# Spreading the base projection over 24 attention passes and turning the second LoRA block in pass 11

## The reference, cut to what matters

```python
qk = (x @ Wqk_w.T + Wqk_b).reshape(b, n, H, E, 2)          # H = 8 heads of E = 8
scores = jnp.einsum('bhqd,bhkd->bhqk', q, k)
attn = jax.nn.softmax(scores, axis=-1) / HEAD_DIM ** 0.5
out = jnp.einsum('bhsl,bhlv->bhsv', attn, v)
...
h = jnp.einsum('nd,erd->ner', x_flat, A)                    # 8 experts of rank 16
hw = h * combine[:, :, None]
expert_out = jnp.einsum('ner,eor->no', hw, B) * SCALING
base_out = x_flat @ W_base.T + b_base
out = base_out + expert_out
```

## Time and profile before

| what | value |
|---|---|
| time, median of three runs | 1461.27 us (1458.69 to 1462.09) |
| the profiled execution: its time, its span | 1458.69 us, 1456.6 us |
| busy over the span | PE 1370.9, DVE 980.3, ACT 855.1, POOL 633.5 us |
| passes 0 to 31, from 78 to 211 us | 133 us, of which PE 121.8, DVE 83.2, ACT 79.8, POOL 49.4 us busy |
| granted clock of PE in that stretch | 0.94 on the mean |

### The profile page before, as it was taken

How to read it: one execution, slowest core, us unless ns; L and a number is a source line. 1 busy time by engine, 2 the same in 40 slices (tenths; PEclk the granted TensorE clock), 3 DMA queues, 4 the chain that set the end, 5 groups by cost and what they waited for, 6 DMA issues and landing times.

```text
span 1456.6 us, 21333 instructions
## 1 busy us (share of the span) xinstructions
PE 1370.9 (94%) x7350; PEld 1075.4 (74%) x7350; DVE 980.3 (67%) x1834; ACT 855.1 (59%) x2103; POOL 633.5 (43%) x973
## 2 busy tenths in 40 slices
PE   4989897999999999999999999999999999989997
PEld 3743345788888788877888888788878877768786
DVE  6666655677777777768777777767677777675333
ACT  2355564566666666666666657666666666563211
POOL 4333345444454454434454544544344545433211
PEclk9999888999999999999999999999999999999999
DMA  4200032001110020102011100201020012114010
GB/s 142 66 1 1 2 100 69 30 1 59 36 40 31 30 67 9 39 22 74 5 56 35 39 31 30 68 7 45 16 74 20 26 35 38 38 59 136 15 58 29
DMA packets 35882, 61.01 MB, mean 42 GB/s; under 512 B 9056, under 2 KB 13280, under 8 KB 35776
## 3 DMA queue, kind: packets, MB, share of 16 engines
q1 hardware_dynamic: 35776, 59.66, 13.0%
HBM read 49.68 MB, written 9.96 MB: 41 GB/s over the span
## 4 chain that ended last, share of the span: by engine, by line
PE 75%; DVE 12%; issue 7%; ACT 3%; POOL 2%; DMA 1%; POOLq 0%; DVEq 0%; SPq 0%; ACTq 0%
PE T L2302 7%; PE T L1917 7%; PE T L1919 6%; PE T L1918 6%; PE S L1919 5%; PE S L1918 5%; PE S L1917 5%; PE VB L1919 4%; PE VB L1917 4%; PE WB L1917 4%; PE VB L1918 4%; PE WB L1919 4%; PE WB L1918 4%; PE VB L2073 2%; PE T L2185 2%
## 5 line engine op out<-in xcount | busy, mean ns | idle before, releaser
L892 POOL TENSOR_TENSOR RI<-SM,C 128x1 f32<-128x1 f32 x256 | 143.3, 560 | 506.6 <-ACT PB L1222 505.4
L1689 DVE CUSTOM_DVE_ANT_0 PB<-S,REL,SLC 128x128 f32<-128x128 f32 (+7 forms) x256 | 204.4, 813 | 80.1 <-PE S L1919 78.5
L1222 ACT ACTIVATE PB<-PB,NM 128x128 f32<-128x128 f32 (+7 forms) x256 | 198.9, 777 | 69.0 <-DVE NM L1689 64.1
L1295 ACT ACTIVATE R<-T 128x512 fp32r<-128x512 f32 x288 | 170.6, 593 | 100.4 <-PE T L2302 98.4
L893 POOL TENSOR_SCALAR PB<-PB,RI 128x128 f32<-128x128 f32 (+7 forms) x256 | 214.9, 839 | 25.2
L1696 DVE TENSOR_TENSOR R<-T,R 128x512 fp32r<-128x512 f32 x288 | 197.4, 688 | 42.2 <-ACT R L1295 23.7
L2302 PE MATMUL T<-C,PB 128*128 128x128 f32 x1152 | 176.6, 276 | 12.0 <-DVE R L1696 6.8
L2302 PEld LDWEIGHTS T<-C,PB 128*128 128x128 f32 x1152 | 134.1, 140 | 48.1 <-DVE R L1696 18.1
L1202 ACT ACTIVATE JUNK<-WB 128x128 bf16<-128x128 f32 x252 | 66.2, 277 | 92.5 <-PE WB L1919 92.5
L1917 PE MATMUL T<-R 128*128 128x512 f32 x256 | 103.9, 406 | 4.0 <-issue 2.2
L1919 PE MATMUL T<-R 128*128 128x512 f32 x256 | 100.4, 392 | 0.0
(11 more groups left out here) (295 smaller groups left out, 3513.7 us busy)
## 6 DMA issues: line engine op xcount, KB each, us to landing
RAW<-w SPq DMA_DIRECT2D x86, 256.0 KB, 2.8
DQ<-codes SPq DMA_DIRECT2D x16, 352.0 KB, 3.5
DQ<-absmax SPq DMA_DIRECT2D x16, 352.0 KB, 3.0
dequantised<-DQ SPq DMA_DIRECT2D x16, 352.0 KB, 2.2
PB<-x SPq DMA_DIRECT2D x12, 256.0 KB, 3.2
PB<-dequantised SPq DMA_DIRECT2D x5, 512.0 KB, 4.6
PB<-x_scratch SPq DMA_DIRECT2D x8, 256.0 KB, 4.0
out<-PB SPq DMA_DIRECT2D x8, 256.0 KB, 2.0
```

The lines of the kernel that those rows point to most:

```text
L892: ch.link(e.tensor_tensor(RI[:, k:k + 1], SM[:, k:k + 1], C[:, C_EXP + 5:C_EXP + 6], ALU.pow))
L1222: e.activation(pb(m, a, 0, L), pb(m, a, 0, L), ACT.Exp, scale=-1.0, bias=NM[:, k:k + 1], accum_out=SM[:, k:k + 1]).then_inc(exp_done, 1)
L1295: e.activation(r(PT + AT[i, ("PV", kb)] % 3 * 1024, 512), T[AT[known, it] % 2][:, :], ACT.Copy).then_inc(t_act, 1)
L1689: e.tensor_tensor_reduce(out=pb(m, a, 0, L), in0=bank[:, 0:L], in1=REL[:, TOK - L:TOK], scale=SLC[:, a:a + 1], scalar=3.0e38, op0=ALU.add, ...
```

## The change

The base projection was packed more densely into passes 0 to 5, and blocks 3 to 7 followed three passes each until pass 20. Now each block takes three passes from the start, with 5, 5 and 2 pieces, and the last one ends in pass 23. XB moves from pass 0 to pass 11, which has no pieces, and from bank VB to bank WB, between the blocks 3 and 4. The first PV waits only for group 0. Two items of the merged list stand ahead of ST 1 and the rest behind it, and this holds for the head items from pass 24 on as well. SH moves to the end of its pass. The gating of block t-1 on POOL moves to HN t, and that of the last block from pass 22 to pass 24.

```diff
@@ -100,26 +100,16 @@
 EARLY = 4
 W_AT = {}
-for _x in [("F", t) for t in range(NT)] + [("WO", t) for t in range(NT)] + [("PQ", 1)]:
+for _x in ([("F", t) for t in range(EARLY)] + [("XB", 0)] + [("F", t) for t in range(EARLY, NT)] + [("WO", t) for t in range(EARLY)]
+           + [("WO", t) for t in range(EARLY, NT)] + [("PQ", 1)]):
     W_AT[_x] = len(W_AT)
-FILL_X = 22
+FILL_X = 24
 BASE_PRE = 6
...
-FILL = {0: (_pieces(0, 6, 7), _pieces(0, 8, 9, 10, 11)),
-        1: ([("HN", 0)], _pieces(1, 0, 1, 2)),
...
-for _t in range(3, NT):
-    FILL[3 * _t - 3] = _pieces(_t, 0, 1), _pieces(_t, 2, 3, 4)
-    FILL[3 * _t - 2] = _pieces(_t, 5, 6), _pieces(_t, 7, 8, 9)
-    FILL[3 * _t - 1] = _pieces(_t, 10, 11), [("HN", _t)]
+_b = [("B", 0, m) for m in range(3 * KT)]
+FILL = {0: _b[BASE_PRE:10], 1: _b[10:] + [("HN", 0)], 11: [("XB", 0)]}
+for _t in range(1, NT):
+    _b, _x = [("B", _t, m) for m in range(3 * KT)], 3 * _t - (1 if _t < EARLY else 0)
+    FILL.update({_x: _b[:5], _x + 1: _b[5:10], _x + 2: _b[10:] + [("HN", _t)]})
...
@@ unit_items
-    pre, post = FILL.get(x, ([], []))
+    fill = FILL.get(x, []) + head_items(x - EARLY_X)
     first, second, extra = couples(x) if x <= 23 else (None, None, None)
     seq = [("ST", 0)] + ([first] if first else []) + ([("PV", x - 1)] if x else [])
-    seq += pre + [("ST", 1)] + ([second] if second else []) + ([("XB", 0)] if x == 0 else [])
-    if x in (7, 15, 23):
-        return seq + [("SH", x // NT + 1)] + post + head_items(x - EARLY_X)
-    return seq + post + head_items(x - EARLY_X) + ([extra] if extra else [])
+    seq += fill[:2] + [("ST", 1)] + ([second] if second else []) + fill[2:] + ([extra] if extra else [])
+    return seq + ([("SH", x // NT + 1)] if x in (7, 15, 23) else [])
@@ POOL
                         add_bias0(it[1])
-                    elif it[0] == "B" and it[1] and it[2] == 7:
-                        gate0(it[1] - 1)
+                        if it[1]:
+                            gate0(it[1] - 1)
@@ high_hn (ACT)
-                act.wait_ge(xa_full, g + 1)
-                e.activation(r(OT + g * 1024, 512), VB[:, :], ACT.Copy).then_inc(xa_high, 1)
+                if g == 0:
+                    act.wait_ge(xa_full, 1)
+                else:
+                    act.wait_ge(w_full, W_AT["XB", 0] + 1)
+                e.activation(r(OT + g * 1024, 512), (VB, WB)[g][:, :], ACT.Copy).then_inc((xa_high, xb_high)[g], 1)
@@ low_hn (DVE)
-                dve.wait_ge(xa_high, g + 1)
+                dve.wait_ge((xa_high, xb_high)[g], 1)
                 o = OT + g * 1024
-                e.tensor_tensor(r(o + 512, 512), VB[:, :], rf(o, 512), ALU.subtract).then_inc(xa_low, 1)
+                e.tensor_tensor(r(o + 512, 512), (VB, WB)[g][:, :], rf(o, 512), ALU.subtract)\
+                    .then_inc((xa_low, w_free)[g], 1)
@@ values0, turn_hn (PE)
                 if x == 0:
-                    pe.wait_ge(xa_low, 2)
+                    pe.wait_ge(xa_low, 1)
...
                 if g == 1:
-                    pe.wait_ge(xa_low, 1)
+                    pe.wait_ge(w_free, W_AT["XB", 0])
                 pe.wait_ge(hn_ready, 4 * g + 4)
                 for t in range(4):
-                    last = e.transpose(VB[:, t * P:(t + 1) * P], HN[:, (4 * g + t) * P:(4 * g + t + 1) * P], IDENT)
-                last.then_inc(xa_full, 1)
+                    last = e.transpose((VB, WB)[g][:, t * P:(t + 1) * P], HN[:, (4 * g + t) * P:(4 * g + t + 1) * P], IDENT)
+                last.then_inc((xa_full, w_full)[g], 1)
```

More of the change, by code:

```diff
@@ L102 @@
 W_AT = {}
-for _x in [("F", t) for t in range(NT)] + [("WO", t) for t in range(NT)] + [("PQ", 1)]:
+for _x in ([("F", t) for t in range(EARLY)] + [("XB", 0)] + [("F", t) for t in range(EARLY, NT)] + [("WO", t) for t in range(EARLY)]
+           + [("WO", t) for t in range(EARLY, NT)] + [("PQ", 1)]):
     W_AT[_x] = len(W_AT)
-FILL_X = 22
+FILL_X = 24
 BASE_PRE = 6
-def _pieces(t, *ms):
-    return [("B", t, m) for m in ms]
-FILL = {0: (_pieces(0, 6, 7), _pieces(0, 8, 9, 10, 11)),
-        1: ([("HN", 0)], _pieces(1, 0, 1, 2)),
[L115 to L118, removed]
-for _t in range(3, NT):
-    FILL[3 * _t - 3] = _pieces(_t, 0, 1), _pieces(_t, 2, 3, 4)
-    FILL[3 * _t - 2] = _pieces(_t, 5, 6), _pieces(_t, 7, 8, 9)
-    FILL[3 * _t - 1] = _pieces(_t, 10, 11), [("HN", _t)]
+_b = [("B", 0, m) for m in range(3 * KT)]
[3 more added lines that the diff above has]
+    FILL.update({_x: _b[:5], _x + 1: _b[5:10], _x + 2: _b[10:] + [("HN", _t)]})
 PAIRS = 16
@@ L548, in program @@
         xa_low = sem("xa_low")
+        xb_high = sem("xb_high")
         m_high = sem("m_high")
@@ L1152, in sums0 @@
                 if u == 3:
-                    act.wait_ge(xa_full, 2)
+                    act.wait_ge(w_full, W_AT["XB", 0] + 1)
                 e.activation(SUMS[u], VB[:, :], ACT.Copy).then_inc(sums_ready, 1)
@@ L2079, in turn_hn @@
                 if g == 1:
-                    pe.wait_ge(xa_low, 1)
+                    pe.wait_ge(w_free, W_AT["XB", 0])
                 pe.wait_ge(hn_ready, 4 * g + 4)
                 for t in range(4):
-                    last = e.transpose(VB[:, t * P:(t + 1) * P], HN[:, (4 * g + t) * P:(4 * g + t + 1) * P], IDENT)
-                last.then_inc(xa_full, 1)
+                    last = e.transpose((VB, WB)[g][:, t * P:(t + 1) * P], HN[:, (4 * g + t) * P:(4 * g + t + 1) * P], IDENT)
+                last.then_inc((xa_full, w_full)[g], 1)
             def experts(t):
-                pe.wait_ge(xa_low, t // 4 + 1)
+                if t < EARLY:
+                    pe.wait_ge(xa_low, 1)
+                else:
+                    pe.wait_ge(w_free, W_AT["XB", 0] + 1)
                 pe.wait_ge(split, W0_EXP)
```

## The result

| kernel | median of 5 runs | profiled execution | its span | mean granted clock |
|---|---|---|---|---|
| before | 1458.69 us (1457.42 to 1462.09) | 1458.69 us | 1456.6 us | 0.985 |
| changed | 1468.36 us (1464.19 to 1469.68) | 1465.94 us | 1464.0 us | 0.984 |

The changed kernel is slower: ratio 1.0053, 95% interval 1.0037 to 1.0069. The forecast was 1461.7 us with a range up to 1465. The profiled spans differ by 7.4 us. The summary page doesn't say where: busy PE is 1373.5 us (1370.9 before), and the mean clock is the same. So I lined up the start of PV in every pass. The table has the distance from one PV to the next where the two kernels differ, in us; row x ends at the PV of pass x.

The account below looks back on a forecast made before the run. It took PE, busy 94% of the span, and its handovers with DVE to bound the kernel. Terms summed to -0.9 us, plus 1.3 for the clock in pass 11: +0.4, 1461.7 us, range 1458.0 to 1465.0.

Parts of the forecast that it names:

- the clock in pass 11: Around pass 11, without 128x128 matmuls except transposes: a short fall to half clock more likely than not, +1.3 us (0 to +2.5).
- The others had no more than DVE covers: 0: Passes 2 to 5 other than pass 4: moving pieces changes nothing, since DVE's reductions hide them; 0 us.
- SH with "+0.05" in pass 15: SH moved to the end of passes 7 and 15: +0.05 us for each, together +0.1.
- the tail counted "at nothing": Tail and layer 1, after this stage: they follow its end unchanged, counted at nothing.
- the second rival: Clock falls in pass 11 and stays down as between 173 and 190: +5.4 us, 1466.7 us; chance 0.09.
- The first rival: The clock holds in pass 11: -0.9 us, 1460.4 us; chance 0.28.
- XB's stall by itself: Pass 11: reductions queue behind XB's remainder on DVE, first MM to first MM 4.8 us instead of 4.0, +0.8.
- Passes 24 and 25: With pieces up to pass 23 the clock holds here: 7.1 us instead of 9.75, -2.6 (0 to -3.0).
- the third rival: Clock falls in passes 24 and 25 nevertheless, giving back the 2.6 us: +1.7, 1463.0 us; chance 0.11.
- Passes 27 to 31: End of the stage: ST 1 behind more work makes PV wait for ACT's exponential; +1.45 us in sum.
- The fourth rival: The late ST 1 costs nothing, exponentials still ready in time: -2.8 us and less, 1458.4 us; chance 0.11.
- The +0.4 for the last gate: Last gate on POOL, moved to pass 24, delays a weight remainder, load and ACT copy: +0.4 us (0 to +1.7).

Follow-up runs that it names:

- the second profile: The changed kernel run once more with no edit, beside the kernel before on the same chip: 1468.82 us, ratio 1.0032 against the kernel before.
- full array work in pass 11: Changed kernel plus five unread 128x128 matmuls of 512 columns ahead of the second MM of pass 11, XB staying there: 1463.8 us, ratio 1.0009 against the kernel before.
- gate back: Changed kernel with the gating of block t-1 put back on piece 7 of block t on POOL: 1465.06 us, ratio 1.0024 against the kernel before.
- the experiment with the head items: Changed kernel with all head items put behind ST 1 again: 1462.34 us, ratio 1.0 against the kernel before.
- the first run with full array work at every place: Changed kernel, gating back on piece 7, five unread 128x128 matmuls each in pass 11 and ahead of passes 3 and 5: 1462.34 us, ratio 1.0011 against before.

## Why the prediction was wrong

The forecast was +0.4 us on the profiled execution. At the last PV there are +5.3 (5.86 less the 0.53 of the start), and +1.5 in the tail. Four terms of the sum failed: the clock in pass 11 (+1.3, measured 3.6), "The others had no more than DVE covers: 0" (measured +1.53 in pass 3), SH with "+0.05" in pass 15 (measured +1.52), and the tail counted "at nothing" (+1.5). With a fall in passes 5 and 6 as in the second profile it is 3.7 more.

**The clock in pass 11.** The fall was forecast, and the term was mis-sized: +1.3 was taken, 3.6 measured. The price of half clock was about right (3.6 of 10.2 us is 35%, or 38% with the 0.3 us at the end of pass 11; 37% was worked out). The length was not. I took half of the shortest stretch in the trace, because dense pieces follow at once. They followed, and the clock stayed down for 10.2 us, about the figure that the second rival named as its limit. That rival had 0.09 and came nearest in time (1466.7 against a profiled 1465.94 and a median of 1468.36), but this is luck in the main: it had 17.0 us at half clock for 6.3 us, and the passes 3 and 15 and the tail, of which it says nothing, made up the rest. The reason against a long fall, the five pieces in each pass, was a reason without a row.

The wait of PE, which the prediction counted among the reasons of the fall ("PE idles 2 us of it"), isn't needed for it. The first rival, and with it the rule of the Trainium skill (TensorE: Matmul & The Clock Gate, section "HAM oscillation — how this bites in real kernels"), which puts the loss down to a long idle wait, fails: the clock fell with the wait for XB, and with it taken away it fell with no idle time above 1.14 us. What that rival had in its favour was misread, too: between 190 and 211 there are not "only short matmuls and transposes" but four output projections, each with two matmuls of 128x128 by 512. The Trainium skill has a second way on the same page, in the section "A second HAM failure mode: psum-queue depth-cycling": short idle times between groups of matmuls, coming often. The runs here agree with that only in part: with PE busy for 3.05 of 3.5 us the clock fell (32 rows), and with 2.27 of 3.4 us it held (full array work in pass 11), the smaller share of the two.

**"The others had no more than DVE covers: 0" in passes 2 to 5.** This is the step that failed by neglect. The sum was made of time alone. Pass 2 lost two of seven pieces, which cost nothing and gained nothing in time, but they were full array work in a pass of 5.9 us. PE then waited 1.37 us for DVE, as before, and pass 3 ran at half clock for 3.4 us: +1.53. Five matmuls that nothing reads, ahead of pass 3, held the clock there. Pass 4 itself came out as forecast (-0.35, -0.33 forecast). Passes 5 and 6 can fall in the same way, as the second profile shows; the first was spared it.

**The gate on POOL.** I weighed one gate of eight, the last, and gave SH +0.1 in all. The gate of block 3 moved to HN 4 at the end of pass 14, and there it stands behind a bias and ahead of the shift of round 2. Pass 15 costs +1.5. Both directions were run: gate back, 4.85; gate alone in the old kernel, 6.66. In pass 7 the bias comes behind the shift (115.13 and 113.02), and nothing is lost (4.85 in both kernels). The order of POOL follows from the list of items like that of PE and DVE, and the prediction followed only those two there.

**What was right.** Passes 0 and 1: -0.71 (-0.7). XB's stall by itself: 4.70 us from first MM to first MM, forecast 4.8, so +0.7 (+0.8), by the queue of DVE as described. Passes 24 and 25 keep their clock: -2.37 (-2.6), and the third rival didn't come. That was in part luck: with the same items in these passes the clock fell at 188.4 in the first run with full array work at every place. Passes 27 to 31: +1.72 where +1.45 was forecast; the experiment with the head items takes 1.64 of it away. The fourth rival is refuted by the same run. The +0.4 for the last gate does not show: with the head items behind ST 1, ACT's weight copies waited 0.92 and 0.54 us for their transfers, and pass 27 took 3.20 us, as before. Passes 21 to 23: -0.62 (-0.1), somewhat better.

**What stays open.** That the tail follows unchanged failed in this execution by 1.5 us, in one fall at 245.5. Whether it is due to the change, or to where the tail happens to stand, wasn't tested. Why passes 24 to 31 keep the clock in some executions and lose it in others is open as well, and so is what sets the length of a fall. With the three terms of the stage put right the sum is -0.9 + 3.6 + 1.5 + 1.5 = +5.7, near the measured +5.3; the whole time of single runs varies by more.

## What to carry to other kernels

When filler work is spread out or moved, ask of each place it leaves what it did besides its time: here 128x128 matmuls beside 32-row and 32-column ones kept the clock up, and the pass without them cost 3.6 us at half clock, where the wait in it cost 0.7. Look at every queue that the moved item passes, at every repetition of it, not only the last. And before trusting a difference of a few microseconds from five runs, see whether one stretch of the kernel has two lengths.

## What the runs showed of the hardware

That matmuls which nobody reads can make a kernel faster: 12 of them, ratio 0.9954. That in this stage the rows of the array in use count, and not busy time alone: with the same 12 at 32 rows, and PE busy for 3.05 of 3.5 us, the clock fell for 41 us. And that a fall, once it has come, lasted 3.4, 6.8, 10.2, 13.7, 17.0, 27.4 or 41 us; at half clock a busy PE (39.02 of 41.1 us, 40.50 of 41.0) didn't get it back soon where the passes held mostly narrow matmuls, and five pieces a pass didn't bring it back at once either (10.2 us in passes 12 and 13). In one and the same kernel the same fall took 17.0 us in one execution and 41.1 in another, and that makes 9.2 of the 10.1 us between these two.
